# Two layer norms around linear attention and a spiking feed-forward: the second norm folded into up-weights and per-token thresholds

## What is computed

```
x  : 8 x 1024 tokens of 256 values, f32
x1 = x + attention(layernorm(x))
  Q, K, V = xn wq^T, xn wk^T, xn wv^T         (64 wide)
  energy  = K^T V  per batch (64 x 64)
  attention = (Q energy) * sqrt(3/64) wo^T
out = x1 + feed_forward(layernorm(x1))
  h = square(relu(x1n W_fc^T))                (1024 wide)
  y = h W_proj^T                              (256 wide)
  five steps: mem = 0.9 mem + y - (mem > 1);  spk = mem > 1
  result = sum of spk / 5
layernorm(v) = (v - mean) / sqrt(var + 1e-5), over the 256 values
```

## Time and profile before

| | before |
|---|---|
| median of three runs | 482.85 us |
| the profiled execution, its own time | 483.47 us |
| its span, first to last instruction | 481.7 us |
| mean granted TensorE clock | 0.994 |
| busy PE / PEld | 466.1 (97%) / 420.1 (87%) us |
| busy DVE / ACT / POOL | 364.7 (76%) / 285.5 (59%) / 236.8 (49%) us |

### The profile page before, as it was taken

The page is one execution under the profiler, slowest core; times in us unless marked ns, Lnnn a source line. Parts: engine busy times, 40 slices in busy tenths (PEclk is TensorE's granted clock), DMA queues, the critical chain, the costliest instruction groups (busy, mean ns, idle before and its releaser), DMA issues.

```text
span 481.7 us, 8498 instructions
## 1 busy us (share of the span) xinstructions
PE 466.1 (97%) x3004; PEld 420.1 (87%) x3004; DVE 364.7 (76%) x982; ACT 285.5 (59%) x519; POOL 236.8 (49%) x196
## 2 busy tenths in 40 slices
PE   7699899999999999999999999999999999999995
PEld 6588698998999989898998989899989989999995
DVE  4767758887878879787879878787888875939447
ACT  4518665756575665756666575666657565656540
POOL 1724556373655447374554637355453734445440
PEclk9999999999999999999999999999999999999999
DMA  8513021050503204050311305041210101010102
GB/s 283 142 46 74 15 44 46 11 122 2 131 2 75 57 37 97 1 132 0 82 51 55 79 1 132 1 91 42 59 30 1 45 1 46 0 45 1 46 12 77
DMA packets 60714, 26.63 MB, mean 55 GB/s; under 512 B 55552, under 2 KB 56192, under 8 KB 60416
## 3 DMA queue, kind: packets, MB, share of 16 engines
q1 hardware_dynamic: 60672, 26.09, 20.6%
HBM read 17.69 MB, written 8.39 MB: 54 GB/s over the span
## 4 chain that ended last, share of the span: by engine, by line
PE 89%; DVE 7%; DMA 1%; issue 1%; ACT 1%; SPq 0%; POOL 0%; DVEq 0%; ACTq 0%
PE y_ps L817 12%; PE y_ps L816 12%; PE y_ps L815 12%; PE hid_ps L815 12%; PE hid_ps L816 12%; PE hid_ps L817 12%; PE work_ps L857 3%; PE work_ps L926 1%; PE work_ps L925 1%; DVE cnt L716 1%; PE work_ps L893 1%; PE kv_ps L815 1%; DMA xs<-x_dram 1%; PE kv_ps L816 1%; PE kv_ps L817 1%; PE e_ps L906 1%
## 5 line engine op out<-in xcount | busy, mean ns | idle before, releaser
L341 POOL TENSOR_TENSOR hid_l<-hid,hid_h 128x512 fp32r<-128x512 f32 x128 | 165.2, 1295 | 211.8 <-ACT hid_h L395 211.6
L384 ACT ACTIVATE relu<-hid_ps 128x512 f32<-128x512 f32 x128 | 76.6, 598 | 113.0 <-PE hid_ps L817 112.6
L817 PE MATMUL y_ps<-wdn_h,hid_l 128*128 128x256 f32 x480 | 135.7, 283 | 0.0
L816 PE MATMUL y_ps<-wdn_l,hid_h 128*128 128x256 f32 x480 | 135.6, 283 | 0.0
L815 PE MATMUL y_ps<-wdn_h,hid_h 128*128 128x256 f32 x480 | 135.1, 282 | 0.0
L815 PE MATMUL hid_ps<-x2T_h,wup_h 128*128 128x512 f32 x256 | 105.4, 412 | 0.4 <-DVE x2T_l L634 0.4
L816 PE MATMUL hid_ps<-x2T_l,wup_h 128*128 128x512 f32 x256 | 100.7, 393 | 0.0
L817 PE MATMUL hid_ps<-x2T_h,wup_l 128*128 128x512 f32 x256 | 100.1, 391 | 0.0
L815 PEld LDWEIGHTS y_ps<-wdn_h,hid_h 128*128 128x128 f32 x480 | 91.4, 190 | 5.1
L816 PEld LDWEIGHTS y_ps<-wdn_l,hid_h 128*128 128x128 f32 x480 | 91.5, 191 | 4.9
L817 PEld LDWEIGHTS y_ps<-wdn_h,hid_l 128*128 128x128 f32 x480 | 91.4, 191 | 0.0
(11 more groups left out here) (127 smaller groups left out, 612.3 us busy)
## 6 DMA issues: line engine op xcount, KB each, us to landing
xs<-x_dram SPq DMA_DIRECT2D x15, 512.0 KB, 4.1
out_dram<-x SPq DMA_DIRECT2D x15, 512.0 KB, 2.9
x_block<-x_dram SPq DMA_DIRECT2D x104, 64.0 KB, 2.7
hid<-w_up_dram SPq DMA_DIRECT2D x1, 1024.0 KB, 8.1
x<-w_down_dram SPq DMA_DIRECT2D x1, 1024.0 KB, 10.2
xs<-x_dram SPq DMA_DIRECT2D x2, 256.0 KB, 3.4
out_dram<-x SPq DMA_DIRECT2D x1, 256.0 KB, 2.0
out_dram<-x SPq DMA_DIRECT2D x2, 128.0 KB, 1.9
```

The source lines that it names most:

```text
L341: nc.gpsimd.tensor_tensor(hid_l[:, i % 2, c, :], hid[:, c % 4, :], hid_h[:, i % 2, c, :].bitcast(f32), ALU.subtract).then_inc(hid_ready, 1)
L384: nc.scalar.activation(relu[:, c % 2, :], hid_ps[c % 2][:, :], ACT.Relu).then_inc(relu_done, 1)
L816: mm(dst, a[0], b[1], start=False, stop=False)
L817: return mm(dst, a[1], b[0], start=False, stop=stop)
```

## The change

The second norm is taken out of the feed-forward: relu squared of (x1 - mean)/dev is relu squared of (x1 - mean) over dev squared. So the up-weights are centred over their 256 inputs on the chip at the start (mean by a matmul with `averager`, subtraction by VectorE in four pieces), TensorE turns x1 as it is, and y is compared with threshold times (variance + eps), a `bound` of five values per token (`moments(n, 1)`, one VectorE instruction of 128x20 after the aggregation, one step later than before). GpSimd's power and VectorE's normalise of the second norm fall away. `turned` is now used for x alone.

At the same time the order of a step is changed: energy_sum goes to chunk 0, energy_times_wo to 1, attend to 2, project_kv to 4, turn_kv to 5; the turn of x1 stays at 6 (at 4 in step 0). The low half of kv goes from VectorE to GpSimd for groups 4 and up, kv_scale moves between the two halves of the spikes, residual ahead of the first norm's statistics. On SP the store and the load now stand ahead of the block loads. In the start the up-weights' high and low halves follow the centring, and the 20 rounds of keep_warm after the two energy sums become 9. The diff, cut to what is spoken of:

```diff
-                if there(r, i + RING) and not (isinstance(r, int) and i < 0):
-                    load_blocks(r, i + RING)
+                if there(r, i - 2):
+                    store(r, i - 2)
                 if there(r, i + RING + 1):
                     load(r, i + RING + 1)
-                if there(r, i - 1):
-                    store(r, i - 1)
+                if there(r, i + RING) and i >= 0:
+                    load_blocks(i + RING)
...
+            def low_half_of_up(h):
+
+                pool.wait_ge(wup_high, h + 1)
...
+            def kv_low_half(r, n):
+
+                pool.wait_ge(kv_high, upto(r, n + 1))
+                src = kv_scaled[:, :].rearrange("p (a d) -> p a d", d=HEAD)
+                high = kv[:, :, :, 0, :].rearrange("p t s d -> p (t s) d")
+                low = kv[:, :, :, 1, :].rearrange("p t s d -> p (t s) d")
+                nc.gpsimd.tensor_tensor(low, src, high.bitcast(f32), ALU.subtract).then_inc(kv_ready, 1)
...
-                        inverse_deviation(r, 2 if is_first(r, i) else i + 3, 0)
-                    if c == 4 and there(r, i + 1):
-                        inverse_deviation(r, i + 1, 1)
+                        inverse_deviation(r, 2 if is_first(r, i) else i + 3)
+                    if c == 7 and there(r, i + 3) and not is_first(r, i):
+                        kv_low_half(r, i + 3)
...
+                if i == 0 and c == 1:
+                    act.wait_ge(wup_ready, 2)
...
+            def high_half_of_up(h):
+
+                act.wait_ge(wup_centred, 2 * h + 2)
...
...
+                    if c == 5:
+                        x2T_high_half(0, 1)
                     if c == 6:
                         kvT_out(0, 3)
-                        x2T_high_half(0, 1)
...
+                        if c == 0:
+                            energy_first_half(r, i + 2)
                         if c == 1:
-                            energy_first_half(r, i + 2)
-                        if c == 2:
                             eo_high_half(r, i + 2)
                     if c == 1 and there(r, i + 3):
                         xT_high_half(r, i + 3)
+                    if c == 4 and there(r, i + 3):
+                        kvT_out(r, i + 3)
                     if c == 6 and there(r, i + 3):
-                        kvT_out(r, i + 3)
+                        kv_high_half(r, i + 3)
                     if c == 6 and there(r, i + 1):
                         x2T_high_half(r, i + 1)
                 if there(r, i):
                     high_half(r, i, FC - 1)
-                if there(r, i + 3):
-                    kv_high_half(r, i + 3)
 
...
-            half_of_columns(w_loaded["up"], wup_raw, wup_h, wup_high, 0)
             kvT_out(0, 0)
+            kv_high_half(0, 0)
             q_high_half(0, 0)
-            half_of_columns(w_loaded["up"], wup_raw, wup_h, wup_high, 1)
             kvT_out(0, 1)
-            kv_high_half(0, 0)
+            high_half_of_up(0)
+            kv_high_half(0, 1)
             q_high_half(0, 1)
-            kv_high_half(0, 1)
+            energy_first_half(0, PER_BATCH - 1)
             half_of_columns(w_loaded["down"], wdn_raw, wdn_h, wdn_high, 0)
-            energy_first_half(0, PER_BATCH - 1)
+            eo_high_half(0, PER_BATCH - 1)
+            high_half_of_up(1)
             half_of_columns(w_loaded["down"], wdn_raw, wdn_h, wdn_high, 1)
-            eo_high_half(0, PER_BATCH - 1)
             x2T_high_half(0, 0)
             steps(act, step)
 
...
+            def centre_up(h, k):
+
+                dve.wait_ge(wup_mean, h + 1)
+                rows = wup_raw.rearrange("p (k n) -> p k n", k=EC)[:, k, h * HID // 2:(h + 1) * HID // 2]
+                nc.vector.tensor_tensor(rows, rows, hid_ps[h][:, :], ALU.subtract).then_inc(wup_centred, 1)
+
+            def moments(n, which):
+
+                if which:
+                    b = 2
+                    if n:
+                        dve.wait_ge(bound_ready, n)
+                else:
+                    b = n % 2
+                    if n >= 2:
+                        dve.wait_ge(rstd_ready, n - 1)
                 for t in range(TILES):
-                    if t == TILES // 2 and isinstance(r, int) and n == 0 and which == 0:
+                    if t == TILES // 2 and n == 0 and which == 0:
...
-            def normalise(r, n):
-                dve.wait_ge(rstd_ready[1], upto(r, n + 1))
-
...
-                for t in range(TILES):
-                    cols = slice(t * EMB, (t + 1) * EMB)
-                    last = nc.vector.tensor_scalar(x2n[:, cols], x1[:, n % RING, cols], mv[1][:, t, 0:1],
-                                                   rstd2[:, t:t + 1], ALU.subtract, ALU.mult)
...
+                if which:
+                    if n == 0:
+                        dve.wait_ge(theta_ready, NUM_STEPS)
+
+                    nc.vector.scalar_tensor_tensor(
+                        bound[:, n % RING, :, :], mv[b][:, :, 1:2].broadcast_to([P, TILES, NUM_STEPS]), EPS,
+                        theta[:, :].unsqueeze(1).broadcast_to([P, TILES, NUM_STEPS]), ALU.add, ALU.mult).then_inc(bound_ready, 1)
+                else:
+                    nc.vector.tensor_scalar(ve[b][:, :], mv[b][:, :, 1], EPS, None, ALU.add).then_inc(moments_ready, 1)
 
             def residual(r, n):
...
+                def limit(level):
+                    return bound[:, n % RING, 2 * pair + a, level:level + 1]
...
+                        nc.vector.tensor_scalar(acc, y, limit(0), None, ALU.is_gt).then_inc(count_step, 1)
                     elif level < NUM_STEPS:
-                        nc.vector.scalar_tensor_tensor(acc, y, THETA[level], acc, ALU.is_gt, ALU.add)\
+                        nc.vector.scalar_tensor_tensor(acc, y, limit(level), acc, ALU.is_gt, ALU.add)\
                             .then_inc(y_free if o == PAIR_OPS - 3 else count_step, 1)
...
                 residual(0, 1)
-                moments(0, 1, 1)
                 q_low_half(0, 2)
                 kv_scale(0, 2)
                 kv_low_half(0, 2)
-                normalise(0, 1)
                 x2T_low_half(0, 1)
                 first_moments(0, 3)
+                moments(0, 1)
                 kv_scale(0, 3)
                 kv_low_half(0, 3)
...
+                if there(r, i + 1):
+                    residual(r, i + 1)
                 if there(r, i + 3):
                     first_moments(r, i + 3)
-                if there(r, i + 1):
-                    residual(r, i + 1)
-                    moments(r, i + 1, 1)
+                if there(r, i):
+                    moments(i, 1)
                 if is_last(r, i - 1):
                     for t in range(TILES):
                         last_spikes(t)
                     return
                 if there(r, i - 1):
                     spikes(r, i - 1, 0, range(0, PAIR_OPS // 2))
-                if there(r, i + 1):
-                    normalise(r, i + 1)
+                if there(r, i + 3):
+                    kv_scale(r, i + 3)
                 if there(r, i - 1):
                     spikes(r, i - 1, 0, range(PAIR_OPS // 2, PAIR_OPS))
                 if there(r, i + 1):
                     x2T_low_half(r, i + 1)
-                if there(r, i + 3):
-                    kv_scale(r, i + 3)
-                    kv_low_half(r, i + 3)
 
 
             centre_weights(w_loaded["kv"], wkv_raw[:, :], 0, wkv_centred)
             first_moments(0, 1)
             kv_scale(0, 0)
+            centre_up(0, 0)
...
             kv_scale(0, 0)
+            centre_up(0, 0)
             kv_low_half(0, 0)
             kv_scale(0, 1)
+            centre_up(0, 1)
             kv_low_half(0, 1)
             q_low_half(0, 0)
             energy_sum(0, PER_BATCH - 1)
             q_low_half(0, 1)
             eo_low_half(0, PER_BATCH - 1)
+            centre_up(1, 0)
+            centre_up(1, 1)
             residual(0, 0)
-            moments(0, 0, 1)
-            normalise(0, 0)
             x2T_low_half(0, 0)
             steps(dve, step)
                 last.then_inc(mean_done, 1)
 
...
-            def turn_second(r, n):
-
+            def turn_x1(n):
+
+                pe.wait_ge(x1_ready, n + 1)
                 for t in range(TILES):
-                    if t % 2 == 0:
-
-                        pe.wait_ge(x2n_ready, upto(r, n, 2, t // 2 + 1))
                     for k in range(EC):
                         at = t * EMB + k * P
-                        last = nc.tensor.transpose(turn2_banks(r, n)[k][:, t * P:(t + 1) * P], x2n[:, at:at + P],
+                        last = nc.tensor.transpose(x1_banks(n)[k][:, t * P:(t + 1) * P], x1[:, n % RING, at:at + P],
                                                    ident[:, :])
-                last.then_inc(x2n_turned, 1)
+                last.then_inc(x1_turn, 1)
+
+            def average_up(h):
+
+                pe.wait_ge(w_loaded["up"], 16)
+                pe.wait_ge(xT_ready, 2)
```

(41 more changed lines are left out.)

115 lines of the change are left out of this document (55 added, 60 removed).

## The result

The changed kernel takes 486.61 us (median of seven, 486.05 to 487.09); the kernel before, timed beside it, 484.55. The ratio is 1.0054, interval [1.0041, 1.0068]: slower by 2.6 us (the medians alone lie 2.1 apart). The forecast was +0.7 us, with most weight on no difference that can be told. The time lies in the stated range, but the kernel is slower, clear of noise. The profiled executions are 483.47 and 487.05 us, spans 481.7 and 485.2: 3.5 us apart, more than the ratio gives.

The account below looks back on a forecast made before the run. TensorE bounds the kernel from 60 us, leaving gains only in start, step 0 and end. Terms -1.1 + 0.1 + 0 + 1.7 = +0.7 gave 484.2 us on the profile, 483.5 on the median; range 479.3 to 487.0.

Parts of the forecast that it names:

- the clock term: Start: TensorE's longer wait before the energy sum leaves later work at 1.2 GHz, up to 1.9 us, taken as 0.85.
- The steady steps: Steps after step 1: TensorE's instruction count is unchanged and no wait opens, taken as 0.
- three covers: Steady steps: margins shrink but hold: x2T_low about 0.65, kv_low_half 1.2 or more, eo_low_half about a microsecond.
- Rival (3): Steady steps: kv_low_half on GpSimd takes over 2.5, TensorE waits at chunk 0 in twelve steps, +4.8, 488.3 us; chance 0.20.
- The end: Last tiles: comparisons with a pointer cost 67 ns more, 1.3 in the last chain plus 0.4 before it, +1.7 us.
- Rival (1): End: a pointer costs nothing in the comparisons, the term is 0, 481.8 us; chance 0.18.
- Step 0 and step 1: Step 1 begins 2.4 us earlier, but TensorE waits 2.4 for kv at the energy sum: +0.1, bounds -0.7 and +0.8.
- Rival (2): Step 1: the wait for kv does not form, so step 0's 2.4 us stay, 481.1 us; chance 0.22.
- The start: Until the first up-projection: normalising removed, up-weight centring added, clock loss counted: -1.1 us, bounds -1.95 and 0.
- the 4.2 to be removed: Start, residual's end to up-projection: 7.29 us becomes 3.1 as TensorE turns x1 itself, removing 4.2.
- The chain: Start: mean, centring and kv halves put the energy sum near 23.5, residual at 29.15, paying back 2.25 us.
- rival (4): Start: not shortened at all, clock down until attention, 484.6 us; counted within the forecast's chance of 0.40.

Follow-up runs that it names:

- run 1: Changed kernel with comparisons reading immediates again, the per-token bounds still computed: 485.14 us, ratio 1.0023 to the kernel before.
- run 2: Kernel before, with its five fixed thresholds read from a tile in SBUF by pointer: 485.45 us, ratio 1.0028.
- run 5: Kernel before, with the energy sum at chunk 0, energy-times-wo at 1 and attention at 2 in step 1 alone: 486.89 us, ratio 1.0078.
- run 3: Changed kernel with step 1 alone in the old order, energy sum at chunk 1: 482.64 us, ratio 0.9969 to the kernel before.
- run 6: Changed kernel with the second up-weight mean between the start's two energy sums, two keep_warm rounds in its old place: 485.66 us, ratio 1.0042.
- run 8: Changed kernel without the mean and centring of the up-weights: 482.91 us, ratio 0.9969 to the kernel before.
- run 9: Changed kernel with the edits of run 3 and run 7, and the second mean replacing two keep_warm rounds behind the second energy sum: 478.13 us, ratio 0.9880.
- run 10: Run 9 with the first energy sum ahead of the first mean and the first two centring pieces behind the energy: 477.23 us, ratio 0.9861.
- run 7: Changed kernel with the kv halves ahead of the up-weights in the start, on TensorE, VectorE and ScalarE: 483.80 us, ratio 0.9994.

## Why the prediction was right and wrong

Two steps of the prediction failed, and the price of the clock is in both. In the start the clock term was put at 0.85, bounded by 1.9, and measured 2.3. In step 1 a term for the clock behind the wait was left out without a reason, and it measured 1.5. On the profiled pair the start came out 1.6 us dearer than forecast and steps 0 and 1 1.3 dearer.

- **The steady steps (taken as 0): right.** All three covers held, two of them to a tenth of a microsecond. Rival (3) fell: GpSimd does kv's low half in 1.30, as it does hid_l.
- **The end (+1.7): right.** Measured +0.45 and +1.21. The pointer's 67 ns, read from two rows with other operators, is 60 to 61 in runs 1 and 2, which change nothing else, and they show it from both sides. Rival (1), a free pointer, fell. The formula of the Trainium skill's page "VectorE: DVE Perf Modes", section "The TRN2 errata", has a fixed part and the element count and no term for where a scalar comes from; the rows have one.
- **Step 0 and step 1 (+0.1, bounds -0.7 and +0.8): this term failed.** The wait itself was right, 2.42 for 2.4, and run 5 has it alone; the gain of step 0 was 2.77 for 2.4. What was left out is what came behind the wait: 3.4 us at the lower clock, 1.5 us more. The prediction had weighed that for the start and not here. Measured +1.41. Rival (2), that the wait doesn't form, is what run 3 makes true by an edit: 4.1 us.
- **The start (-1.1, bounds -1.95 and 0): mis-sized, and outside its bounds.** Of the 4.2 to be removed, 4.1 went, and more than that was paid back: +0.47. The chain was right link by link up to kv's low half, and the energy sum came at 23.73 for 23.5. The clock term failed. The prediction's own sign, a clock below full from 22 to 29 us, came true, but was priced at 0.85. From the energy sum to the centring of the second half it has 4.25 us (23.5 to 27.75); measured are 6.51 (23.73 to 30.24), 2.3 more. In between stand eight transposes in 1.93 us, energy-times-wo in 1.06 and the second mean in 2.98; run 6, whose clock stayed full, has 1.06, 0.70 and 1.93 for them. This is rival (4), with a little more. A bound of "no gain" was no bound.

Luck has a part in the clock terms. The profile of the kernel before has its clock low for 3.4 us in the start and the changed kernel's for 6.8; but run 5, whose start is the old one, has 6.8 too, and its up-projection comes 0.6 us later after the first kv projection than before (25.31 for 24.74). So a share of the +0.47 belongs to the execution and not to the change.

On the 2.42: the Trainium skill, "SBUF — State Buffer", section "Who interferes with whom", says that a VectorE instruction with two SBUF inputs contends with a GpSimd instruction that reads SBUF, and that the port pair they share is an exclusive lock. The rows fit it: GpSimd's 2.34 began at 20.79 and ended at 23.13, VectorE's began at 21.26 and ended at 23.68, 0.55 later. So its duration was set by the end of GpSimd's instruction. In the kernel before it was the same: GpSimd's instructions ended at 17.82 and 20.59, VectorE's kv low halves at 18.36 and 21.14, 0.54 and 0.55 later, and in run 8 19.80 and 20.35. The prediction took the durations 1.25 to 1.65 from these rows; what carries over is the distance between the two ends.

With the measured parts the sum is +0.5 +1.4 +0 +1.7 = +3.6 on the profiled pair. The medians are closer together because the profiled execution of the kernel before lies 1.1 under the median of the seven timed beside the changed kernel, and the one after 0.4 over its own (mean clock 0.984, where its six others have 0.987 to 0.990). The kernel before has executions with a mean clock of 0.994, as the profiled one, and more with 0.991 or 0.992, most of which take longer.

## What to carry to other kernels

When an operand's preparation leaves the critical chain, look what the new preparation stands in front of on every engine: here 4.2 us of normalising were exchanged for centring that stood ahead of kv, and kv was the chain. A product moved one slot earlier needs the cover of its slowest input in the first step, where the pipeline isn't full, and not only in the steady one. And count a stall of TensorE twice, once for itself (2.6 us here) and once, with a chance, for the clock behind it (1.5). Work that is wanted anyway, here the second mean, was worth putting into the hole: by itself it is unclear (run 6), and in runs 9 and 10, beside the other two remedies, the clock stayed full.

## What the runs showed of the hardware

- A VectorE comparison on 128x256 with one scalar read from SBUF took 60 to 61 ns more than with an immediate in the same kernel, for tensor_scalar (415 to 475, 410 to 471) and scalar_tensor_tensor (413 to 473, 410 to 471) alike.
- The 128x512 subtraction of two SBUF operands took 0.69 us alone and up to 2.42 beside GpSimd's 128x1024. Where GpSimd's was at work first, the subtraction ended 0.54 to 0.55 us after GpSimd's. The small bound instruction on 128x20 took between 228 and 1192 ns in the changed kernel; why isn't shown.
- TensorE's clock fell to its lower level (1.2 of 2.4 GHz) at 63.5 us, after a wait of 2.42 that had ended at 61.8, and 20 transposes in place of that wait kept it up. All five profiles of the changed kernel and its variants in which this wait stands open (the result's and those of runs 1, 6, 7 and 8) have such a drop; in the old kernel's copy of the wait the clock stayed up in the profiled execution.
- The f32 matmul of 512 columns shows as two matmul records, which at full clock began 0.43 us apart, where one fp32r matmul of that size follows the next after 0.23. Two such matmuls took 1.93 us.
